# Four-kilobyte runs for the experts' gate and up weights, with the stored rows' channels in the matching order

## The reference

```
xn    = (x - mean) / sqrt(var + 1e-5)
attn  = einsum(feats, weights), both of them c * exp(dot products with proj_matrix - norm term), 512 features
logits = xn @ router_w          # 64 experts in 8 groups; best 4 groups, then the best 8 experts of a token
dispatch[e, position] = xn[token]              # at most 256 tokens for an expert, in order of arrival
y[e]  = (silu(dispatch[e] @ gate_w[e]) * (dispatch[e] @ up_w[e])) @ down_w[e]    # 512 -> 256 -> 512
out   = x + attn + sum over a token's experts of weight * y[e] + shared expert(xn)   # the same form, dense
```

## Time and profile before

| what | value |
|---|---|
| median of 3 runs | 1309.34 us (1308.23 to 1309.87) |
| the profiled execution's own time | 1307.97 us |
| its span | 1306.2 us |
| lies around the span | 1.8 us |
| TensorE (PE) busy | 1280.0 us, 98% of the span |
| VectorE (DVE), ScalarE (ACT), GpSimd (POOL) busy | 70%, 50%, 33% |
| granted TensorE clock, mean | 0.996 of full speed |
| DMA | 203800 packets, 263.65 MB, mean 202 GB/s |

### The profile page before, as it was taken

The page is one execution under the profiler, slowest core; times in us unless marked ns, Lnnn a source line. Parts: engine busy times, 40 slices in busy tenths (PEclk is TensorE's granted clock), DMA queues, the critical chain, the costliest instruction groups (busy, mean ns, idle before and its releaser), DMA issues.

```text
span 1306.2 us, 22561 instructions
## 1 busy us (share of the span) xinstructions
PE 1280.0 (98%) x7565; PEld 1123.8 (86%) x7565; DVE 916.0 (70%) x1787; ACT 647.3 (50%) x1053; POOL 433.9 (33%) x344
## 2 busy tenths in 40 slices
PE   6999999999999999999999999999999999999995
PEld 5888888888888888888889999999999999999994
DVE  7878877777777777785656667667766766676662
ACT  4421232212322123221256777777877777777772
POOL 1000000000000000000014666777666667676653
PEclk9999999999999999999999999999999999999998
DMA  7336554664546645445447999999999999999995
GB/s 269 121 107 163 130 121 127 157 166 98 130 119 153 167 104 131 114 118 134 134 133 214 286 278 286 287 290 292 290 291 285 298 291 287 282 295 285 298 277 65
DMA packets 203800, 263.65 MB, mean 202 GB/s; under 512 B 49268, under 2 KB 138744, under 8 KB 203768
## 3 DMA queue, kind: packets, MB, share of 16 engines
q1 hardware_dynamic: 175096, 191.93, 50.9%
q0 software_dynamic: 28672, 71.32, 23.7%
HBM read 178.18 MB, written 71.39 MB: 191 GB/s over the span
## 4 chain that ended last, share of the span: by engine, by line
PE 96%; DVE 2%; DMA 1%; ACT 0%; issue 0%; POOL 0%; SPq 0%; ACTq 0%
PE pmm L1255 18%; PE pmm L1257 18%; PE pmm L1256 18%; PE pout L1255 11%; PE pout L1257 11%; PE pout L1256 11%; PE ptr L1488 4%; PE plog L1316 2%; PE plog L1325 1%; PE ptr L1267 0%; DMA out_dram<-outs,slot_cols 0%; DVE stats L829 0%; DMA xbuf<-_L_attn_proj_matrix_dram 0%; DVE xt_lo L795 0%; PE plog L1345 0%
## 5 line engine op out<-in xcount | busy, mean ns | idle before, releaser
L1614 POOL DMA_INDIRECT out_dram<-outs,slot_cols x128 | 228.7, 1787 | 165.6 <-DMA out_dram<-outs,slot_cols 136.2
L1255 PE MATMUL pmm<-xt_hi,proj_hi 128*128 128x256 f32 (+1 forms) x784 | 253.0, 323 | 2.2 <-DVE xt_lo L795 1.4
L1257 PE MATMUL pmm<-xt_hi,proj_lo 128*128 128x256 f32 (+1 forms) x784 | 249.6, 318 | 0.0
L1256 PE MATMUL pmm<-xt_lo,proj_hi 128*128 128x256 f32 (+1 forms) x784 | 249.6, 318 | 0.0
L1255 PE MATMUL pmm<-xt_hi,sgu_hi 128*128 128x256 f32 (+1 forms) x768 | 246.1, 320 | 0.2 <-issue 0.2
L1256 PE MATMUL pmm<-xt_lo,sgu_hi 128*128 128x256 f32 (+1 forms) x768 | 243.4, 317 | 0.0
L1257 PE MATMUL pmm<-xt_hi,sgu_lo 128*128 128x256 f32 (+1 forms) x768 | 243.4, 317 | 0.0
L1598 POOL TENSOR_TENSOR earlier<-earlier,chosen 128x64 bf16<-128x64 bf16 x64 | 23.9, 373 | 617.8 <-DVE chosen L916 614.0
L1604 POOL DMA_INDIRECT xbuf<-rows,slot_cols x128 | 175.3, 1369 | 80.8 <-issue 38.6
L552 ACT ACTIVATE feat<-pmm,ab 128x512 f32<-128x512 f32 x68 | 46.7, 687 | 292.4 <-PE pmm L1257 286.4
L1255 PEld LDWEIGHTS pmm<-xt_hi,proj_hi 128*128 128x128 f32 x784 | 147.3, 188 | 13.6 <-ACT feat L552 1.6
(11 more groups left out here) (185 smaller groups left out, 2543.7 us busy)
## 6 DMA issues: line engine op xcount, KB each, us to landing
raw<-in_L_ffn_gate_w_dram SPq DMA_DIRECT2D x64, 512.0 KB
raw<-in_L_ffn_up_w_dram SPq DMA_DIRECT2D x64, 512.0 KB
raw<-in_L_ffn_down_w_dram SPq DMA_DIRECT2D x64, 512.0 KB
outs<-in_L_attn_x_dram SPq DMA_DIRECT2D x32, 512.0 KB, 3.9
out_dram<-outs SPq DMA_DIRECT2D x32, 512.0 KB, 3.0
xbuf<-in_L_attn_x_dram SPq DMA_DIRECT2D x52, 256.0 KB, 7.6
raw<-xn SPq DMA_DIRECT2D x52, 256.0 KB, 6.2
rows<-raw SPq DMA_DIRECT2D x39, 256.0 KB, 4.2
```

The costliest lines, as they stand in the source:

```text
L1255: pe.matmul(psum, lh, rh, start=first and n == 0, stop=False)
L1256: pe.matmul(psum, lh, rl, start=False, stop=False)
L1257: ins = pe.matmul(psum, ll, rh, start=False, stop=final and n == len(pairs) - 1)
L1614: pool.indirect_dma_start(out=out, out_offset=bass.IndirectOffsetOnAxis(ap=slot_cols[:, at:at + 1], axis=0), in_=outs[e.b][:, c, :], in_of ...
```

## The change

- The experts' gate and up weights are loaded as `(p c) i`: block c of partition p is channel 4p + c, one run of 4 KB for each partition and matrix.
- The stored rows get their channels in the same order. ScalarE copies `xn` into free parts of `raw`, reading every fourth element, four copies of 128x512 for a group and two small ones for channel 0 from `xn_first` (`copy_rows`). SyncE stores from there (`store_rows`), two DMAs in groups 0 to 2 and eight in the others, in runs of 2 KB. `store_xn` and `store_xn_quads` go.
- `normalise` waits for `rows_copied` (the copies) in place of `xn_stored` (the stores). The copies wait for `rows_stored` of the group before.
- In ScalarE's order the copies of group 0 stand before `features(0, 3)`, those of group 1 after `hidden(g, 0)` of group 0, those of group 2 before `hidden(g, 1)` of group 1, and all others at the end of a group, after `exp_logits(nxt)`. In SyncE's order the stores stand before `store_out(g, 1)`; in the first two groups the loads around them change places.

```diff
             def load_half(b, m, weights):
                 sp.dma_start(raw[b][:, at].rearrange("p (c i) -> p c i", c=HB),
-                             weights.rearrange("(c p) i -> p c i", p=P)).then_inc(gu_loaded[b][m], 16)
+                             weights.rearrange("(p c) i -> p c i", p=P)).then_inc(gu_loaded[b][m], 16)
...
+        def row_place(g, a):
+            if isinstance(g.n, int) and g.n < 2:
+                return raw[1][:, 2 * a * H:2 * (a + 1) * H].rearrange("p (j h) -> p j h", j=2)
+            return raw[a][:, GU:].rearrange("p (j h) -> p j h", j=2)
...
-            def store_xn(g):
...
-            def store_xn_quads(g):
...
+            def store_rows(g):
+                sp.wait_ge(rows_copied, 2 * (g.n + 1))
+                for a in range(2):
+                    at = slice(2 * a, 2 * a + 2)
+                    if isinstance(g.n, int) and g.n < STD:
+                        sp.dma_start(rows_groups[g.n][:, at, 0:H], row_place(g, a)).then_inc(
+                            rows_stored, 16)
+                    else:
+                        for q in range(P // SQ):
+                            sp.dma_start(rows_quads[g.n, q][:, at, 0:H], row_place(g, a)[q:P:P // SQ]).then_inc(
+                                rows_stored, 16)
...
             def group(g, more_x=True):          # SyncE, groups 2 to 13
                 load_residual(g)
                 load_quad(later)
                 if more_x:
                     load_x_quads(Turn(g.i + 2, g.b))
-                store_xn_quads(later)
                 store_counts(g)
                 store_out(g, 0)
                 store_w(nxt)
+                store_rows(later)
                 store_out(g, 1)
...
             def first_group(g):                 # SyncE
-                store_xn(nxt)
-                load_x_quads(turn(3))
                 sp.wait_ge(shared_less_made, 2)
                 sp.wait_ge(router_less_made, 1)
                 load_residual(g)
+                store_rows(nxt)
+                load_x_quads(turn(3))
...
+            def copy_rows(g):                   # ScalarE
+                act.wait_ge(norm_made, g.n + 1)
+                if isinstance(g.n, int) and g.n <= STD:
+                    if g.n == 1:
+                        act.wait_ge(rows_stored, 32)
+                    if g.n == 2:
+                        act.wait_ge(shared_lo_made, 3)
+                    if g.n == 3:
+                        act.wait_ge(rows_stored, ROWS_STD)
+                else:
+                    act.wait_ge(rows_stored, ROWS_STD + ROWS_QUAD * (g.n - STD))
+                std = isinstance(g.n, int) and g.n < STD
+                for a in range(2):
+                    for i in range(2):
+                        j = 2 * a + i
+                        to = row_place(g, a)[:, i]
+                        if std:
+                            ins = act.activation(to.rearrange("p (c q) -> p c q", c=HB),
+                                                 xn[:, j].rearrange("p (q c) -> p c q", c=HB), copy)
+                        else:
+                            ins = act.activation(to.rearrange("p (c b i) -> p c b i", c=HB, b=HB),
+                                                 xn_quarters[:, :, j].rearrange("p b (i c) -> p c b i", c=HB), copy)
+                    ins.then_inc(row_step, 1)
+                    act.wait_ge(row_step, 2 * g.n + a + 1)
+                    act.activation(row_place(g, a)[:, :, 0], xn_first[:, 2 * a:2 * a + 2], copy).then_inc(rows_copied, 1)
...
             features(0, 2, wt_hi, scale=ab2[:, 2:3])
             for half in range(2):
                 hi_half(2, half, xt_hi[0], (pout2, ptr)[half])
+            copy_rows(turn(0))
             features(0, 3, wt_hi, scale=ab2[:, 3:4])
...
             def normalise(g, base):             # VectorE
                 if isinstance(g.n, int) and g.n <= STD:
                     dve.wait_ge(turned, 2 * (g.n + 2))
-                    at_least(dve, xn_stored, 32 * g.n)
                 else:
                     dve.wait_ge(quad_loaded, 16 * HB * (g.n - STD))
-                    dve.wait_ge(xn_stored, XN_STD + XN_QUAD * (g.n - STD))
+                at_least(dve, rows_copied, 2 * g.n)
```

More of the change, by code:

```diff
@@ L49 @@
 STD = 3
-XN_STD = 32 * STD
-XN_QUAD = 16 * (HB + P // SQ)
+ROWS_STD = 32 * STD
+ROWS_QUAD = 16 * 2 * (P // SQ)
 ROW = H + E
@@ L258, in build @@
         norm_made = sem("norm_made")
-        xn_stored = sem("xn_stored")
+        rows_stored = sem("rows_stored")
+        rows_copied = sem("rows_copied")
+        row_step = sem("row_step")
         quad_loaded = sem("quad_loaded")
@@ L378, in load_quad @@
                     sp.dma_start(quad[b * SQ:(b + 1) * SQ, :], xn_quarters[:, b]).then_inc(quad_loaded, 16)
-            def store_xn_quads(g):
-                sp.wait_ge(quad_loaded, 16 * HB * (g.n - STD + 1))
-                for b in range(HB):
-                    at = slice(1 if b == 0 else 0, P)
-                    sp.dma_start(rows_squares[g.n][:, :, b * P + at.start:(b + 1) * P],
-                                 quad[b * SQ:(b + 1) * SQ, :].rearrange("p (k c) -> p k c", c=P)[:, :, at]).then_inc(
-                        xn_stored, 16)
-                for q in range(P // SQ):
-                    sp.dma_start(rows_quads[g.n, q][:, :, 0:1], xn_first[q:P:P // SQ].unsqueeze(2),
-                                 allow_slow_non_contiguous=True).then_inc(xn_stored, 16)
             def store_w(g):
@@ L442, in second_group @@
                 nxt, later = g.next(), Turn(g.i + 1, g.b)
-                store_xn(nxt)
+                load_residual(g)
+                sp.wait_ge(xn_made, nxt.n + 1)
                 load_x_quads(turn(4))
-                load_residual(g)
+                store_rows(nxt)
+                sp.wait_ge(rows_stored, 32 * 2)
                 load_quad(later)
                 load_x_quads(turn(5))
-                store_xn_quads(later)
                 store_counts(g)
@@ L456, in before_last_group @@
                 load_residual(g)
-                sp.wait_ge(xn_stored, XN_STD + XN_QUAD * (GROUPS - STD))
+                sp.wait_ge(rows_stored, ROWS_STD + ROWS_QUAD * (GROUPS - STD))
                 sp.wait_ge(quad_turned, 2 * (GROUPS - STD))
@@ L495, in _ @@
             sp.wait_ge(iw_sums_turned, 1)
-            store_xn(turn(0))
+            store_rows(turn(0))
             load_x(turn(2))
@@ L643, in gate_up_hi, with group @@
                                    egu_raw[e.b][:, at], copy).then_inc(egu_hi_made[m], 1)
-            def group(g, last=False):
+            def group(g, last=False, copies=True):
                 nxt = g.next()
@@ L669, in group @@
                     exp_logits(nxt)
+                if copies:
+                    copy_rows(Turn(g.i + 1, g.b))
             act.wait_ge(ab_made, 1)
@@ L709, in _ @@
                     group(Turn(i, b))
-            group(turn(GROUPS - 2))
-            group(turn(GROUPS - 1), last=True)
+            group(turn(GROUPS - 2), copies=False)
+            group(turn(GROUPS - 1), last=True, copies=False)
             def down_hi(e):
@@ L1619, in _ @@
             pool.wait_ge(slot_cols_made, 1)
-            pool.wait_ge(xn_stored, XN_STD + XN_QUAD * (GROUPS - STD))
+            pool.wait_ge(rows_stored, ROWS_STD + ROWS_QUAD * (GROUPS - STD))
             pool.wait_ge(w_stored, 16 * GROUPS)
```

9 lines of the change are left out of this document (3 added, 6 removed).

## The result

| | before | after |
|---|---|---|
| median | 1309.24 us (1307.44 to 1366.98, 20 executions) | 1315.47 us (1309.81 to 1350.74, 20 executions) |
| fastest execution | 1307.44 us | 1309.81 us |
| profiled execution, span | 1307.97, 1306.2 us | 1313.28, 1311.5 us |
| DMA packets, MB | 203800, 263.65 | 126488, 263.65 |
| ScalarE busy | 50% | 55% |

The ratio is 1.0044 (95%: 1.0024 to 1.0065): 0.44% slower. The forecast was 1309.5 us, within 0.2% of no change; the result lies outside the range of 1307.0 to 1312.5 as well. Single executions of either kernel ran tens of microseconds longer than the others; ratios here leave such disturbed ones out, medians don't.

What follows compares the result with a forecast made beforehand. TensorE, 96% of the chain that ended last, was taken to bound the kernel, leaving only the ends open. Start +0.4 and tail -0.2 sum to +0.2 us on the median 1309.34: 1309.5 us, range 1307.0 to 1312.5.

Steps and rivals of the forecast that it cites:

- c = 0.6: At the start, the assumed distance in us between starts of two of ScalarE's strided copies of group 0, giving +0.4 us.
- The term for ScalarE's copies of group 0: At the start, copies before `features(0, 3)` delay `wt_lo` and, one for one, TensorE's next product: +0.4 us.
- the bounds 0.53 and 1.0: At the start, limits for c: contiguous ScalarE copy (0.53, +0.1 us) and VectorE's transpose reading every fourth element (+2.0 us).
- 33.22 + 4c: At the start, the predicted time in us when `wt_lo` can start, c being the copies' spacing; 35.24 before.
- Rival 1: At the start, strided copies are dear, c = 1.0: +2.0 us, 1311.3 us with the tail unchanged; chance 0.13.
- The term of 0 for the 4 KB loads: In the experts' stage, longer gate and up runs move bytes no faster and TensorE covers them: 0 us.
- rows 11: Profile rows of q0 beside q1: 5.2 short or 1.1 long q1 packets per q0 packet, read as turns bounded by bytes.
- rival 2: In the experts' stage, longer runs crowd out GpSimd's scatters, `outs` is late for `e_down`: 30 us more, 1339 us; chance 0.07.
- ScalarE's copies from group 1 on: In the first stage, these copies fit in gaps where ScalarE waits, 4.10 to 15.30 us long: 0 us.
- no gain beyond the ends: TensorE has no idle time in the middle, so only the kernel's start and tail can change the time.
- The tail's -0.2 us: At the end, the last scatters to `out` might land earlier; -0.2 us taken between 0 and -1.0.
- Rival 3: At the tail, 4 KB runs do load the engines less, winning the whole 1.0 us: 1308.4 us; chance 0.07.

Runs made afterwards that it cites:

- the extra load in 4 KB runs: The kernel before plus one never-read 512 KB gate load per expert from 3 on, gate, up and extra in 4 KB runs: 1412.64 us, ratio 1.0774.

## Why the prediction was wrong

**The step that failed: c = 0.6.** The term for ScalarE's copies of group 0 was mis-sized: +0.4 us in the sum, 2.1 us measured, c = 1.02 against the bounds 0.53 and 1.0. The mechanism was right to a tenth of a microsecond: 33.22 + 4c gives 35.34 for copies in order (35.33 measured) and 37.30 for the strided ones, 37.50 with the 0.2 us by which this profile was late already (37.48 measured). Rival 1 had this value. The mistake was the choice between the bounds. I went by TensorE's transposes and by ScalarE's copy of every second element and set aside the one row with the right stride, VectorE's 1.01 us per 512. ScalarE picks every second element at 1.15 us per 1024, almost free, and every fourth at 1.11 us per 512; reading in order and writing every 128th costs 1.14. The Trainium skill, Advanced Engine Details and Errata, SBUF Cachelines, drew the line just there: two accesses to each line of 16 bytes are enough, one is not. By this rule the price steps up between every second and every fourth float32 (by that rule, the trace agrees: 1.15 per 1024, then 1.11 per 512).

**A term that was missing: the clock.** The sum held TensorE's wait and nothing behind it. A stall of 2.0 us at TensorE was not over when TensorE went on; its clock was granted at the 1.2 GHz level for some 3.4 us, 1.6 us more. The three profiles of kernels with the strided read have it (0.50 in 48 to 50 us); the scattered write, with the same stall, has not. The experts' stage shows the same under late rows. In the sixteen profiles, from 35 us on to the last products, the clock fell 42 times. Each fall began during a stall of TensorE of 1.9 us or more, or within 1.4 us of its end; none followed the 78 stalls of 0.9 to 1.9 us. Of 46 stalls of 1.9 to 2.8 us 26 were followed by a fall, and of 16 longer ones all. So a stall of 2.0 us went either way here, and what decides isn't known. That the stalls bring the fall is inferred from this order in time; no run changed the stalls alone.

**The term of 0 for the 4 KB loads, and the reading of rows 11.** The experts' stage was costed at 0, "covered by TensorE", and the profile has 1.4 us of late rows there. "The turn seems to be bounded by bytes" was wrong. The 5.2 and 1.1 packets of q1 for each of q0 were means over stretches in which one of the queues often had nothing to send; they measured who had work, not whose turn it was. Half a microsecond with both queues full gives one for one at 1, 2 and 4 KB. So the mechanism of rival 2 exists, for turns of one packet. Its mark, though, was not the first to show: in the changed kernel ScalarE's wait for `out_dram` is 1.0 us (1.5 before), and what shows is TensorE's wait for gathered rows at a few experts. Under the extra load in 4 KB runs both show, ScalarE's with 58.8 us in 35 waits. The Trainium skill, DMA: Bandwidth & Descriptors, Queues, rings and completion order, has an engine drain a packet of some 9 to 17 descriptors from one queue before it turns to the next. Read as a fixed count, as the prediction did, it gave the warning's direction; the trace differs in the count, for its turns are of one run each.

**How much of the time is which.** In the profiled execution: 2.1 us for the copies and 0.2 that was there before them, 1.6 us clock, 1.4 us late rows, together 5.3. Over the executions: copies alone cost 0.25% (3.3 us), both parts 0.44% (5.8 us). The difference, 2.5 us, would be the share of the 4 KB runs, but the intervals overlap, and the 4 KB runs without the dear start give 1.0010, 1.0006 and 1.0022, none apart from 1. Under more load the mechanism is shown. At the kernel's own load it is seen in profiles (1.3, 5.4, 12.8 and 14.1 us of waits in four of the six with 4 KB runs and no extra load, none in the four whose gate and up runs are of 1 KB) and perhaps in the number of long executions, but not with the loads alone, and its size in the median stays open. So does why one execution slips and the next does not.

**What held.** From the product on to the first turn the copies in order take as long as before, to the hundredth. So these terms held: TensorE without a gap in the first stage; ScalarE's copies from group 1 on, the moved stores, `load_x_quads` and `normalise`'s new wait, all at 0; 4 KB runs hardly lighter for the engines; no gain beyond the ends. The tail's -0.2 us is about -0.1 in the profile. Rival 3 isn't seen: the loads alone, at 1309.03 us, win nothing.

**No version beats the kernel before.** The best candidates tie with it: 0.9997 (copies on GpSimd, 1 KB runs) and 0.9998 (down weights in 2 KB runs).

## What to carry to other kernels

Cutting packets is no gain as such. When two queues share the engines, look at a moment in which both have work, and count. If they alternate packet by packet, the run length of the bulk load is the waiting time of the small, urgent transfers, and making bulk runs longer takes bandwidth from them. And when a new access pattern is to be priced between two bounds, the row with the same stride was the better guide here, though from another engine, than the one with half of it. Then add, for a stall of TensorE like these, the clock after it. Moving work to an idle engine has a price as well if a busy one slows beside it. And before two profiles are compared, count both from a mark ahead of the change.

## What the runs showed of the hardware

- DMA engines with two full queues took one packet of each in turn: 37 to 39, 31 to 34 and 23 to 24 in half a microsecond (medians over 304, 155 and 114 of them), with q1's runs of 1, 2 and 4 KB. The queue with packets of 2 KB had 0.81, 0.68 and 0.51 of the engines' time.
- ScalarE copies 128x512 float32 in 0.62 us in order, in 1.11 us reading every fourth element, and in 1.14 us writing every 128th; every second element of 1024 takes 1.15 us. GpSimd takes 1.4 us for the copy with every fourth, and an instruction of VectorE beside it took 1.39 instead of 0.42 us.
- TensorE's granted clock fell to 0.50 for 3.4 us, in two cases for 6.8, after 42 of 62 stalls of 1.9 us or more, and after none of 78 between 0.9 and 1.9 us. At the start of the kernel such a fall cost 1.6 us.
- A round of two scatters and the wait for them took 9.5 us in the kernel before, where an expert takes 9.3 us. A sixth more bytes on the other queue (512 KB beside 1.6 MB at every second expert) went with 35 to 51 us more in four of five executions; one of ten without them was as long.
